# Rows of the first two tiles built inside the table's short chunk, that chunk moved to fifth place, and identity products moved to the table's end

## The reference

```python
scaled = num_value.astype(jnp.float32) / 1000.0
table = jnp.where(is_num[:, None], jnp.sin(scaled[:, None] * freqs[None, :]), weight)   # 12500 x 128
h = table[x]                                   # x: 128 x 128 token ids
h = h + attention(layernorm(h))                # 8 heads of 64, heads mixed before and after the softmax
h = h + ffn(layernorm(h))                      # shared FFN + two banks of 8 experts, top-1, capacity 1280
```

## Time and profile before

| What | Value |
|---|---|
| median of three runs | 1539.84 us (1537.67 to 1542.58) |
| the profiled execution's own time | 1541.32 us |
| its span in the trace | 1539.6 us |
| PE busy | 1482.9 us (96%) |
| DVE, ACT, POOL busy | 1049.7, 1146.7, 971.0 us |
| granted TensorE clock, mean | 0.991 of full speed |

### The profile page before, as it was taken

How to read it: one execution, slowest core, us unless ns; L and a number is a source line. 1 busy time by engine, 2 the same in 40 slices (tenths; PEclk the granted TensorE clock), 3 DMA queues, 4 the chain that set the end, 5 groups by cost and what they waited for, 6 DMA issues and landing times. The chain is left out here.

```text
span 1539.6 us, 33796 instructions
## 1 busy us (share of the span) xinstructions
PE 1482.9 (96%) x11149; PEld 1370.3 (89%) x11149; DVE 1049.7 (68%) x2801; ACT 1146.7 (74%) x3461; POOL 971.0 (63%) x992
## 2 busy tenths in 40 slices
PE   6679999999999999999999999988999999989999
PEld 3368999999999999999999999978999999979999
DVE  7777787787887887787887887764344343346666
ACT  5468888888888888888888888865555555545555
POOL 6665558788878878878878887664677655510000
PEclk9899999999999999999999999999999999999999
DMA  7322321121121111111111111021343234356665
GB/s 254 137 105 98 116 72 50 50 69 41 39 59 38 39 57 35 35 46 44 34 35 54 34 36 51 25 60 42 92 117 102 69 83 111 104 154 184 182 181 148
DMA packets 170603, 126.35 MB, mean 82 GB/s; under 512 B 29539, under 2 KB 154061, under 8 KB 170432
## 3 DMA queue, kind: packets, MB, share of 16 engines
q1 hardware_dynamic: 153024, 104.05, 22.7%
q0 software_dynamic: 17408, 20.16, 4.7%
HBM read 61.63 MB, written 78.56 MB: 91 GB/s over the span
## 5 line engine op out<-in xcount | busy, mean ns | idle before, releaser
L961 ACT ACTIVATE expd<-masked,nmax 128x128 f32<-128x128 f32 x1024 | 395.9, 393 | 0.0
L763 POOL TENSOR_TENSOR prob<-expd,rtotal 128x1024 f32<-128x1024 f32 x128 | 242.9, 1898 | 143.2 <-DVE rtotal L1050 142.1
L1067 DVE COPY_PREDICATED masked<-off_diag,ps_s 128x1024 f32<-128x1024 int32 x128 | 175.2, 1369 | 147.3 <-PE ps_s L857 147.3
L899 PE MATMUL ps_o<-u,probT 128*128 128x128 f32 x2048 | 249.2, 275 | 0.7 <-issue 0.7
L899 PEld LDWEIGHTS ps_o<-u,probT 128*128 128x128 f32 x2048 | 239.1, 192 | 0.9 <-issue 0.9
L961 ACT ACTIVATION_READ_ACCUMULATOR expd<-masked,nmax 128x1 f32 x1024 | 196.9, 192 | 0.0
L970 ACT ACTIVATE u<-ps_ut 128x1024 f32<-128x1024 f32 x128 | 131.5, 1027 | 68.0 <-PE ps_ut L910 68.0
L1082 DVE TENSOR_TENSOR w_lo<-ps_w,w_hi 128x512 fp32r<-128x512 f32 x256 | 164.5, 682 | 3.7 <-ACT w_hi L992 3.6
L985 ACT ACTIVATE probT<-ps_ut 128x1024 f32<-128x1024 f32 x128 | 131.5, 1027 | 45.0 <-PE ps_ut L865 38.4
L992 ACT ACTIVATE w_hi<-ps_w 128x512 fp32r<-128x512 f32 x256 | 146.3, 596 | 18.5 <-PE ps_w L887 12.0
L1073 DVE TENSOR_REDUCE nmax<-masked 128x8 f32<-128x1024 f32 x128 | 155.7, 1216 | 2.5
(11 more groups left out here) (231 smaller groups left out, 3882.2 us busy)
## 6 DMA issues: line engine op xcount, KB each, us to landing
turned<-x2T SPq DMA_DIRECT2D x32, 256.0 KB, 2.2
answers_sp<-zeros SPq DMA_DIRECT2D x16, 512.0 KB
answers_fq<-zeros SPq DMA_DIRECT2D x16, 512.0 KB
xT<-turned SPq DMA_DIRECT2D x56, 128.0 KB, 2.7
sh_back<-answers_sp SPq DMA_DIRECT2D x56, 128.0 KB, 2.3
sh_back<-answers_fq SPq DMA_DIRECT2D x56, 128.0 KB, 2.4
out<-res SPq DMA_DIRECT2D x56, 128.0 KB, 2.0
h_sb<-in_L_tok_weight SPq DMA_DIRECT2D x12, 512.0 KB, 5.6
```

The costliest lines, as they stand in the source:

```text
L763: nc.gpsimd.tensor_tensor(prob[k % 2][:, :].rearrange("p (g j) -> p g j", g=H), expd[k % 2][:, :].rearrange("p (g j) -> p g j", g=H), rtot ...
L899: mm = nc.tensor.matmul(ps_o[:, 0:D], probT[k % 2][:, g * N:(g + 1) * N], u[k % 2][:, g * D:(g + 1) * D], start=(g == 0), stop=(g == H - 1))
L961: ins = nc.scalar.activation(expd[(k - 1) % 2][:, g * N:(g + 1) * N], masked[(k - 1) % 2][:, g * N:(g + 1) * N], ACT.Exp, bias=nmax[(k - 1 ...
L1067: nc.vector.copy_predicated(masked[k % 2][:, :].rearrange("p (g j) -> p g j", g=H), off_diag[:, :].unsqueeze(1).to_broadcast([P, H, N]), p ...
```

## The change

- The table's layout gets two more columns of rows (VX = 100), so that the short chunk has 4 rows, 512 columns. The two new ones are not rows of the vocabulary: they are the rows of the tokens of tiles 0 and 1. SP loads those tokens' ids (`ids0`), POOL gathers their `num_value`, `is_num` and weight rows by six indirect DMAs in the setup, and they go through the same chain as the others. They are never written to the table.
- The short chunk is made fifth (`ORDER`), and the thirteenth place is taken by a full one. The thousandths are made in two parts: the vocabulary's, then the two new columns'. PE starts its first transposes after the first part. The masks' loads go behind the numbers' loads.
- The last chunk's clamp goes from POOL to DVE; ACT's `N_hi` goes ahead of the last two sines; DVE's `M_lo` goes from before the last `reduce` to before the last `put_sines`.
- DVE takes the statistics of tiles 0 and 1 in the setup (at c = 8), POOL their `rstd0` (at c = 9). In the attention, tiles 0 and 1 are no longer gathered: `normalize(0)` is DVE's first row and reads `h_sb`, and the bias is added to the same rows.
- The identity products are 16 instead of 24 and stand at the end of the setup's PE program, behind `reduce` of the twelfth chunk, instead of at the attention's start.

```diff
...
-WARM = 24
+WARM = 16
...
+VX = VS + 2
...
+    ORDER = (0, 1, 2, 3, CHUNKS - 1, *range(4, CHUNKS - 1))
+
     def rows_of(c):
-        return VC if c < CHUNKS - 1 else VS - VC * (CHUNKS - 1)
+        return VC if c < CHUNKS - 1 else VX - VC * (CHUNKS - 1)
...
+            pool.wait_ge(S["ids0"], 16)
+            for t in range(2):
+                nc.gpsimd.indirect_dma_start(num_i[:, VS + t:VS + t + 1], None, num_value.rearrange("(v o) -> v o", o=1),
+                                             bass.IndirectOffsetOnAxis(ap=ids0[:, t:t + 1], axis=0)).then_inc(S["num0"], 16)
...
+            for t in range(2):
+                nc.gpsimd.indirect_dma_start(isn0[:, t:t + 1], None, is_num.rearrange("(v o) -> v o", o=1),
+                                             bass.IndirectOffsetOnAxis(ap=ids0[:, t:t + 1], axis=0)).then_inc(S["rows0"], 16)
+                nc.gpsimd.indirect_dma_start(h_sb[:, (VS + t) * D:(VS + t + 1) * D], None, weight,
+                                             bass.IndirectOffsetOnAxis(ap=ids0[:, t:t + 1], axis=0)).then_inc(S["rows0"], 16)
...
-            for c in range(CHUNKS):
+            for c in range(CHUNKS - 1):
                 clamp(c)
...
+                if c == 9:
+                    link.wait()
+                    pool.wait_ge(S["stat0"], 1)
+                    link(nc.gpsimd.tensor_scalar(C.var[:, 0:2], C.mv1[0][:, 0:2, 1], 1.0, EPS, ALU.mult, ALU.add))
+                    link.inc(nc.gpsimd.tensor_tensor(C.rstd0[:, :], C.var[:, 0:2], C.power[:, 0:2], ALU.pow))
...
-            sp.dma_start(isn[:, 0:VR], is_num[0:P * VR].rearrange("(p r) -> p r", p=P)).then_inc(S["num"], 16)
             sp.wait_ge(S["made"], made["pads"])
             sp.dma_start(num_i[0:REST, VR:VS], num_value[P * VR:VOCAB].rearrange("(p o) -> p o", o=1)).then_inc(S["num"], 16)
-            sp.dma_start(rest_isn[0:REST, 0:1], is_num[P * VR:VOCAB].rearrange("(p o) -> p o", o=1)).then_inc(S["num"], 16)
+            sp.dma_start(ids0[:, :], x[0:2, :].rearrange("b p -> p b"), allow_slow_non_contiguous=True).then_inc(S["ids0"], 16)
+            sp.dma_start(isn[:, 0:VR], is_num[0:P * VR].rearrange("(p r) -> p r", p=P)).then_inc(S["isn"], 16)
+            sp.dma_start(rest_isn[0:REST, 0:1], is_num[P * VR:VOCAB].rearrange("(p o) -> p o", o=1)).then_inc(S["isn"], 16)
...
+            for i, c in enumerate(ORDER):
+                if i == 0:
+                    continue
+                need(sp, s_row[i % 4], loaded.get(i - 4, 0))
...
+            for i, c in enumerate(ORDER):
+                sp.wait_ge(S["done"], i + 1)
+                if c < CHUNKS - 1:
+                    sp.dma_start(t_main[:, cols(c)], h_sb[:, cols(c)]).then_inc(S["put"], 16)
+                else:
+                    sp.dma_start(t_main[:, one], h_sb[:, one]).then_inc(S["put"], 16)
+                    sp.dma_start(table[P * VR:VOCAB, :], h_sb[0:REST, LAST_COL]).then_inc(S["put"], 16)
...
+                if c == CHUNKS:
+                    for half, src in enumerate((ps_t, ps_c)):
+                        act.wait_ge(S["M"], 3 + half)
+                        nc.scalar.activation(mats["N_hi"][:, half * 512:(half + 1) * 512], src[:, :], ACT.Copy).then_inc(S["hi"], 1)
...
-            pe.wait_ge(S["num_f"], 2)
+            pe.wait_ge(S["num_f"], 1)
...
+            pe.wait_ge(S["num_f"], 2)
...
+            pe.wait_ge(S["reduced"], CHUNKS - 1)
+            for _ in range(WARM):
+                nc.tensor.matmul(ps_a[CHUNKS % 2][:, 0:P], ident[:, :], ident[:, :], start=True, stop=True)
...
+            thousandths(slice(0, VS))
+            halves(slice(0, CHUNKS - 1), slice(0, VC))
+            dve.wait_ge(S["num0"], 32)
+            thousandths(slice(VS, VX))
+            halves(slice(CHUNKS - 1, CHUNKS), slice(0, VX - VC * (CHUNKS - 1)))
+            dve.wait_ge(S["isn"], 32)
...
+                if c == CHUNKS - 1:
+                    dve.wait_ge(S["rows0"], 64)
...
                 reduce(c)
+                if c == CHUNKS - 1:
+                    a = angle[c % 3][:, 0:CH]
+                    dve.wait_ge(S["reduced"], CHUNKS)
+                    nc.vector.tensor_scalar(a, a, PI_BELOW, -PI_BELOW, ALU.min, ALU.max).then_inc(S["last"], 1)
...
-                if c == 11:
-                    dve.wait_ge(S["hi"], 1)
-                    link.inc(nc.vector.tensor_tensor(mats["M_lo"][:, :], ps_m[:, :], mats["M_hi"][:, :].bitcast(F32), ALU.subtract))
+                if c == 8:
+                    dve.wait_ge(S["done"], 5)
+                    for t in range(2):
+                        link.inc(nc.vector.bn_stats(C.stat0[:, t, :], h_sb[:, (VS + t) * D:(VS + t + 1) * D]))
+                    link.wait()
+                    for t in range(2):
+                        ins = nc.vector.bn_aggr(C.mv1[0][:, t, :], C.stat0[:, t, :])
+                    ins.then_inc(S["stat0"], 1)
             put_sines(CHUNKS - 2)
+            dve.wait_ge(S["hi"], 1)
+            link.inc(nc.vector.tensor_tensor(mats["M_lo"][:, :], ps_m[:, :], mats["M_hi"][:, :].bitcast(F32), ALU.subtract))
             put_sines(CHUNKS - 1)
...
-            return (i * (BODY // 8) + k // 8 + 1) * 16
+            return (i * (BODY // 8) + k // 8 + (k % 8 >= 2)) * 16
+
+        def rows_in(t):
+            return h_sb[:, (VS + t) * D:(VS + t + 1) * D] if t < 2 else got[t % 8][:, :]
...
-                if k in (-6, -5):
-                    c = slice(2 * k + 12, 2 * k + 14)
-                    need(pool, S["first_stat"], k + 7)
+                if k == -5:
+                    c = slice(2, 4)
+                    need(pool, S["first_stat"], 1)
...
-            for _ in range(WARM):
-                nc.tensor.matmul(ps_o[:, 0:D], ident[:, :], ident[:, :], start=True, stop=True)
...
-                    ins = nc.vector.tensor_scalar(x1[(t0 // 2) % 2][:, b * D:(b + 1) * D], got[t % 8][:, :], mean, rs,
+                    mean = mv1[(t // 4) % 2][:, t % 4, 0:1]
+                    rs = C.rstd0[:, t:t + 1] if t < 2 else rstd[(t // 4 - 1) % 2][:, t % 4:t % 4 + 1]
+                    ins = nc.vector.tensor_scalar(x1[(t0 // 2) % 2][:, b * D:(b + 1) * D], rows_in(t), mean, rs,
...
-                if live(i, k + 8):
+                if 2 <= k + 8 < TILES:
...
-                    if k in (-7, -5):
+                    if k == -5:
                         ins.then_inc(S["first_stat"], 1)
                     elif j == 3:
                         ins.then_inc(S["stat1"], 1)
                     else:
                         link.inc(ins)
-                    if k in (-6, -4):
-                        need(dve, S["first_rstd"], k // 2 + 4)
...
+            normalize(0)
             pipelined(dve, step, BODY, FIRST, LAST, LEAD, END, link, VCHAIN)
...
```

132 lines of the change are left out of this document (66 added, 66 removed).

## The result

| | before | after |
|---|---|---|
| median (lowest to highest), us | 1539.84 (1537.67 to 1542.58, 5 runs) | 1546.06 (1544.86 to 1549.25, 5 runs) |
| profiled execution, us; its span | 1541.32; 1539.6 | 1544.86; 1543.1 |
| next block's first row, SP | 68.66 | 74.74 |
| first `ps_w` / first `ps_s` | 80.74 / 87.21 | 83.65 / 90.66 |
| last `ps_s` of the attention | 1012.24 | 1015.88 |

The ratio is 1.0045, with a 95% interval of 1.0031 to 1.0059: slower by 0.45%. (It is not just the quotient of the two medians, which is 1.0040.) The prediction was 1540.1 with 0.87 on "no change that can be told", and 1546.06 lies above its range.

The account below looks back on a forecast made before the run. PE is busy throughout the attention, so the lead-in before its first products shifts everything behind it. Terms -0.5 + 0.45 + 3.3 - 0.3 - 3.05 + 0.4 = +0.3 us gave a median of 1540.1 us, range 1536.4 to 1543.9.

Parts of the forecast that it names:

- no change that can be told: Whole kernel: median within about 0.3%, 4.6 us, of the kernel before; chance 0.87.
- The table's start: Start of setup: DVE starts earlier, gathered numbers land by 11.0, PE's other transposes go on at 13.2; -0.5 us.
- The bound from the weight loads: Setup start, upper end: gathers as slow as weight loads, 7.5 us, land at 15.0; start term +3.4 us.
- the new numbers come late: Rival, setup start: DVE waits for both gathers, transposes and first sines queue behind; up to 1544.0; chance 0.10.
- Statistics: Table's middle, c = 8: DVE's statistics of tiles 0 and 1 exceed its spare time; +0.45 us.
- The middle: Table's fifth chunk: the shorter chunk's DVE saving is hidden by PE's products; counted as nothing.
- Last chunk: Table's end: full chunk lengthens DVE's last `reduce` and `put_sines` and adds a clamp of 0.8; +3.3 us.
- Close: Last `put_sines` to next block: one 512 KB write replaces two small writes; -0.3 us.
- The head: Attention's start: first `ps_w` comes 9.05 us into the block instead of 12.08; -3.05 us.
- The clock: Attention's start: PE starts at 1.2 GHz and its clock may rise later; +0.4 us.
- The sum: All terms together, whole kernel: +0.3 us, giving a median of 1540.1 us.
- PE's clock rises earlier in the table: Rival, table: full PE rate comes one or two products sooner; up to -3.4 us, 1536.7; chance 0.12.

Follow-up runs that it names:

- a3_short_last: Changed kernel with chunks in natural order: the short chunk last, statistics and `rstd0` of tiles 0 and 1 behind it; ratio 1.0035 to the kernel before.
- a1_warm_back: Changed kernel with 24 identity products back at the attention's start and none at the table's end; ratio 1.0039 to the kernel before.
- g2_after_fourth: The changed kernel, unchanged, run once more in a later batch; ratio 1.0042 to the kernel before.
- c1_after_again: The changed kernel, unchanged, run again beside the kernel before; ratio 1.0049 to the kernel before.
- c0_before_again: The kernel before, unchanged, run against itself; ratio 1.0010.
- f1_before_early_fill: Kernel before with 8 identity products added in PE's gaps ahead of the table's first product; ratio 0.9984 to the kernel before.

## Why the prediction was wrong

- **The table's start** (-0.5; measured +2.43): the step that failed. The term took the gathered numbers to be there at 11.0, early enough for PE to go on at 13.2 instead of 13.79. They came at 13.7, the second chain ended at 16.17 instead of 13.2, and nine transposes stood behind it. DVE's earlier start was even larger than said (3.19 against 3.45). The miss of some 2.7 us in the landing has two parts. The 4.8 us to landing, the slowest of the attention's gathers, were counted from the first gather, but the wait is for both: from the second one, 1.5 us later, the prediction's own rows give 12.5, not 11.0 (+1.5). And the gathers took 6.0 (+1.2). The bound from the weight loads (7.5, landing at 15.0) contained it. The choice of the nearest row by instruction was wrong: all six gathers in this stretch, small pieces as well as rows of 512 bytes, took 4.3 to 6.3 us, so the time most likely went with the traffic, and of that the weight loads' rows told. The rival "the new numbers come late" had the mechanism with a chance of 0.10; by its own rule, slower by over 0.3% only from a landing after 15.4, it does not give the measured time.
- **Statistics** (+0.45): +0.47. **The middle** (0): +0.24; `a3_short_last` shows that the fifth place gives nothing. **Last chunk** (+3.3): +3.02; the clamp took 0.69 instead of 0.8. **Close** (-0.3): -0.08. Here the sum by the Trainium skill's page "DMA: Bandwidth & Descriptors" (section "Anatomy of one DMA"), a term of about 0, came nearer; but the page fits its figure to DMAs that GpSimd issues, and this write is SP's.
- **The head** (-3.05): -3.17; the bias additions stand 10.07 us into the block, predicted 10.2. The size is partly luck: the first gather landed 4.31 us into the block and not 5.65, and the pair waited for the second one, at 5.89.
- **The clock** (+0.4): the first `ps_s` is 3.45 us late, the first `ps_w` 2.91, so +0.54. Right against before. Missed: the shorter head makes the identity products useful, and leaving them would have been worth some 2 us of lead-in (`a1_warm_back`). The Trainium skill's page "TensorE: Matmul & The Clock Gate", cited against this edit, was right in direction.
- **The sum**: +0.3; in the profiled executions +3.5, of which 2.9 are the start's term. With 13.75 in place of 11.0 the forecast would have been about 1543.0, in the range, and still 3 us short of the median.
- **The rest** was in no term. The profiled executions differ by 3.5 us, the medians by 6.2; the profiled one of the changed kernel is its fastest of five. Four batches give 1.0045, 1.0049, 1.0041 and 1.0042, mean 1.0044, or 6.4 to 7.7 us, each with an interval of over 2 us to either side; the last `ps_s` of their traces is 4.0, 3.7, 3.6 and 5.4 us behind 1011.9. One to four us are then left which no trace shows. Two places remain, and neither is shown. The lead-in may be longer in other executions than in the profiled ones, as it is by 1.4 us and more in `g2_after_fourth`; against that as the whole, `a3_short_last` has no lead-in to lose in its trace and is at 1.0035. Or it lies behind the attention. There single traces differ by more than what is sought, with and without the change (from the last `ps_s` to the span's end 561.8 us in `c1_after_again`, 557.8 in `g2_after_fourth`, 565.0 in `c0_before_again`, 556.1 in `f1_before_early_fill`), so traces can't settle it. The place of the buffers was tried (1.0008), the clock in the table too (1.0038). It stays open.
- **The rival "PE's clock rises earlier in the table"** has its sign in the trace: the products of 3.78 us at 35.39 and of 3.59 at 40.25 now take 1.98 and 1.96. But that is not shown to come from the change, since `c0_before_again`, the kernel before, has 1.98 and 1.96 too. It gave nothing: the twelfth `reduce` is still 3.14 us late.
